# First layer of a graph network on one core: dot products by one small addition and repeated weight rows, one copy for a turned block, DVE's operations in another order

## What is computed

```python
def _cg_tp(s, v, y0, y1, w_ss, w_sv, w_vs, w_vv0, w_vv1):
    out_s = concat([w_ss * s * y0, w_vv0 * (einsum('eci,ei->ec', v, y1) / SQRT3)])
    out_v = concat([(w_sv * s)[:, :, None] * y1[:, None, :],
                    w_vs * v * y0,
                    w_vv1 * (cross(v, y1) / SQRT2)])
    return out_s, out_v
```

## Time and profile before

| | |
|---|---|
| median of 3 runs (lowest to highest) | 4406.73 us (4406.34 to 4410.24) |
| the profiled execution, its own time | 4403.17 us |
| its span | 4401.3 us |
| busy share of the span: PE, DVE, ACT, POOL | 82%, 88%, 67%, 62% |
| the first layer's loop, from the first to the last L1282 | 152.9 to 2461.0 us |
| softmax and sums | about 2470 to 2870 us |
| the second layer's loop, matmuls of L926 | 3048 to 4317 us |
| mean granted clock of PE over the span | 0.957 |

### The profile page before, as it was taken

One profiled execution on the slowest core, in us unless ns is written; L12 is line 12 of the kernel. 1 busy time (PEld: TensorE's weight loads), 2 busy tenths in 40 slices (PEclk: granted clock), 3 DMA queues, 4 the chain that ended last, 5 costly groups with the idle time before them and its releaser, 6 DMA issues. The chain is left out here.

```text
span 4401.3 us, 101790 instructions
## 1 busy us (share of the span) xinstructions
PE 3590.4 (82%) x21340; PEld 2663.2 (61%) x21340; DVE 3886.6 (88%) x13162; ACT 2961.6 (67%) x11582; POOL 2707.5 (62%) x2562
## 2 busy tenths in 40 slices
PE   4788888888888888888888477747888888888885
PEld 2678888888888888888888366634333333333334
DVE  7699999999999999999999788855888888888885
ACT  0588888888888888888888322213777776677773
POOL 0576666666666666666666022203888888888881
PEclk9999999999999999999999799956999999999997
DMA  4333333333333333333333188811444444444443
GB/s 146 104 92 88 87 86 88 86 86 88 85 86 88 85 86 88 85 86 88 85 86 88 55 215 220 213 54 53 94 90 88 91 91 88 88 92 91 89 86 92
DMA packets 313045, 426.93 MB, mean 97 GB/s; under 512 B 99333, under 2 KB 248069, under 8 KB 312613
## 3 DMA queue, kind: packets, MB, share of 16 engines
q0 software_dynamic: 141120, 225.15, 23.7%
q1 hardware_dynamic: 171876, 201.27, 14.8%
HBM read 309.10 MB, written 117.09 MB: 97 GB/s over the span
## 5 line engine op out<-in xcount | busy, mean ns | idle before, releaser
L739 POOL DMA_INDIRECT ACC<-hid_tab,idx x784 | 934.7, 1192 | 413.2 <-issue 202.6
L664 POOL DMA_INDIRECT ACC<-src_tab,idx x784 | 823.2, 1050 | 593.3 <-DMA idx<-in_idx_line 377.4
L1106 ACT ACTIVATE ACC<-TR,ACC 128x96 f32<-128x96 f32 (+1 forms) x3136 | 834.4, 392 | 252.2 <-DVE M L1532 237.8
L675 POOL DMA_INDIRECT SC<-dst_tab,idx x784 | 763.1, 973 | 239.1 <-issue 234.5
L789 PE MATMUL TR<-ident,M 128*128 128x128 f32 (+1 forms) x4704 | 650.1, 275 | 263.2 <-issue 214.5
L789 PEld LDWEIGHTS TR<-ident,M 128*128 128x128 f32 (+1 forms) x4704 | 516.3, 137 | 390.0 <-ACT M L1013 328.5
L971 ACT ACTIVATE ACC<-W,ACC 128x64 f32<-128x64 f32 x2352 | 580.9, 342 | 0.0
L838 PE MATMUL HP<-w_hv,MT 128*128 128x128 f32 x3136 | 521.5, 289 | 0.0
L984 ACT ACTIVATE MT<-TR 128x512 f32<-128x512 f32 x784 | 489.4, 624 | 0.0
L813 PE MATMUL E<-w_mv,MT 128*128 128x128 f32 x3136 | 478.9, 275 | 0.0
L926 PE MATMUL E<-M,ohE 128*128 128x480 f32 x784 | 392.7, 626 | 87.8 <-DVE M L1532 86.3
(11 more groups left out here) (220 smaller groups left out, 8216.2 us busy)
## 6 DMA issues: line engine op xcount, KB each, us to landing
h_tab<-ACC SPq DMA_DIRECT2D x392, 160.0 KB, 1.8
SC<-h_tab SPq DMA_DIRECT2D x98, 640.0 KB, 4.5
ACC<-in_e64T SPq DMA_DIRECT2D x98, 256.0 KB
agg_tab<-ACC POOLq DMA_DIRECT2D x98, 240.0 KB
ACC<-src_tab,idx POOLq DMA_INDIRECT x784
SC<-dst_tab,idx POOLq DMA_INDIRECT x784
ACC<-hid_tab,idx POOLq DMA_INDIRECT x784
sum_tab<-ACC POOLq DMA_DIRECT2D x98, 82.0 KB, 4.8
```

The source lines that it names most:

```text
L664: pool.indirect_dma_start(gat0[:, v.slot8, g, :], None, src_tab.ap(), bass.IndirectOffsetOnAxis(ap=idx[:, v.sslot, c:c + 1], axis=0))\
L675: pool.indirect_dma_start(gatd[:, v.slot8, g, :], None, dst_tab.ap(), bass.IndirectOffsetOnAxis(ap=idx[:, v.sslot, c:c + 1], axis=0))\
L739: pool.indirect_dma_start(gat1[:, v.slot8, g, :], None, hid_tab.ap(), bass.IndirectOffsetOnAxis(ap=idx[:, v.sslot, c:c + 1], axis=0))\
L1106: ins = nc.scalar.activation(WS[:, v.par, g, P * k:P * k + hi - lo], wg_[:, lo:hi], ACT.Copy, scale=yg[:, :, k:k + 1].rearrange("p a k -> ...
```

## The change

- **Dot products.** The three products are written straight into M (or M2), 96 columns. One addition adds the first 32 to the second 32 (64 elements over both groups). The third 32 stay as they are, and the weight rows that belong to the dots stand twice in `w_ms0`, `w_hs0` and `ws_val_t` (now 128 rows), so that the matmul adds the last term. `fA` and `fA2` are no longer used.
- **Turned blocks.** The turn takes columns 32 to 416, three blocks of 128. One ACT operation of 768 columns copies them.
- **Loads.** The weight rows are loaded in three parts of five loads each, 15 where there were 9.
- **DVE's order.** `products0` is cut in three: the four products, `rest_of_s0` and `rest_of_v0`; `gated`, `mixed` and `head_values` are cut in two. The order of PE and ACT stays.

```diff
-M0 = 96 + 2 * P
+M0 = C + 3 * P
-B0 = ((0, 96), (96, P), (96 + P, P))
+B0 = ((C, P), (C + P, P), (C + 2 * P, P))
...
-            for r, q in ((slice(0, C), slice(S, 96)), (slice(C, 96), slice(0, S))):
+            for r, q in ((slice(0, C), slice(S, 96)), (slice(C, S), slice(S, 96)), (slice(S, P), slice(0, S))):
                 load(by_head(w_ms0[r, 0:HL])[:, :, 0:16], by_head(a["W_alpha"][q, :]))
                 load(w_ms0[r, HL + C:ES], a["Ws_val"][q, :])
                 load(ws_val_t[:, r], a["Ws_val_T"][:, q])
-            load(w_hs0[:, :], a["Ws_vlin"])
-            load(w2s[0:64, :], rows(a["w2_ss"]))
-            load(w2s[64:96, :], rows(a["w2_vv0"]))
+                load(w_hs0[r, :], a["Ws_vlin"][q, :])
+                load(w2s[r, :], rows(a["w2_ss"] if q.start == 0 else a["w2_vv0"]))
...
-                nc.scalar.activation(dst[0:96, 0].rearrange("p g e -> p (g e)"),
-                                     tr[0:96, 0:G, :].rearrange("p g e -> p (g e)"), ACT.Copy)
-                nc.scalar.activation(dst[:, 1:3].rearrange("p k g e -> p (k g e)"),
-                                     tr[:, G:3 * G, :].rearrange("p a e -> p (a e)"), ACT.Copy).then_inc(LA[sem_done], 1)
+                nc.scalar.activation(dst[:, 0:3].rearrange("p k g e -> p (k g e)"),
+                                     tr[:, 0:3 * G, :].rearrange("p a e -> p (a e)"), ACT.Copy).then_inc(LA[sem_done], 1)
...
-                dots = ch.count(TT(fA[:, :, :, :], feat(S, (C, 3), (1, C)), wgt(160, (64, 3), (1, C)), ALU.mult))
+                dots = ch.count(TT(mid(0, (C, 3), (1, C)), feat(S, (C, 3), (1, C)), wgt(160, (64, 3), (1, C)), ALU.mult))
...
-                TT(mid(C, (S, 2), (1, S)), feat(0, (0, 2), (1, S)), wgt(C, (S, 2), (1, S)), ALU.mult)
-                ch.wait(dots)
-                nc.vector.tensor_reduce(Mt[:, :, 0:C], ax(fA[:, 0, 0, 0:1], (96, G), (1, C), (C, 3)), AX.X, ALU.add)
...
+            def rest_of_s0(v, total, parts):
+                if parts:
+                    mid, feat, wgt, dots, crosses = parts
+                    ch.wait(dots)
+                    TT(mid(C, (1, C)), mid(0, (1, C)), mid(C, (1, C)), ALU.add)
+                    TT(mid(96, (S, 2), (1, S)), feat(0, (0, 2), (1, S)), wgt(C, (S, 2), (1, S)), ALU.mult)
...
+            def mixed_sums(v, total, parts):
+                if parts:
+                    dots, crosses = parts
+                    ch.wait(dots)
+                    TT(M2[:, :, C:2 * C], M2[:, :, 0:C], M2[:, :, C:2 * C], ALU.add)
+                    ch.wait(crosses)
+                    TT(ax(M2[:, 0, 2 * P + C:2 * P + C + 1], (M0, G), (C, 3), (1, C)), fX2[:, :, :, 0, :], fX2[:, :, :, 1, :],
+                       ALU.subtract).then_inc(LA["tp"], 1)
...
             def stage0(t, total):
                 ch.restart()
-                summed = gated(t + -1, total)
+                gated(t + -1, total)
                 added = messages(t + 1, total)
-                scaled(t + -1, total, summed)
-                mixed(t + -1, total)
-                head_values(t + -2, total)
-                products0(t + 1, total, added)
+                ups = gated_up(t + -1, total)
+                parts = products0(t + 1, total, added)
+                done = summed(t + -1, total, ups)
+                scaled(t + -1, total, done)
+                mixes = mixed(t + -1, total)
+                up = head_products(t + -2, total)
+                mixed_sums(t + -1, total, mixes)
+                rest_of_s0(t + 1, total, parts)
+                head_values(t + -2, total, up)
+                rest_of_v0(t + 1, total, parts)
```

More of the change, by code:

```diff
@@ L759, in _ @@
             pe.wait_ge(s_const, 16 * n_loads)
-            nc.tensor.matmul(E1[0:96, 0, 0:C], ws_val_t[:, :], wg[:, :], start=True, stop=True).then_inc(s_wsg, 1)
+            nc.tensor.matmul(E1[:, 0, 0:C], ws_val_t[:, :], wg[:, :], start=True, stop=True).then_inc(s_wsg, 1)
             pe.wait_ge(s_bnd, 1)
@@ L810, in e1 @@
                 for g in range(G):
-                    nc.tensor.matmul(E1[:, 0, ES * g:ES * (g + 1)], MT[0:96, 0, g, :], w_ms0[:, :], start=True, stop=True)
+                    nc.tensor.matmul(E1[:, 0, ES * g:ES * (g + 1)], MT[:, 0, g, :], w_ms0[:, :], start=True, stop=True)
                     for b in range(2):
@@ L835, in hm @@
                 for g in range(G):
-                    nc.tensor.matmul(HP[:, S * g:S * (g + 1)], MT2[0:96, 0, g, :], w_hs0[:, :], start=True, stop=True)
+                    nc.tensor.matmul(HP[:, S * g:S * (g + 1)], MT2[:, 0, g, :], w_hs0[:, :], start=True, stop=True)
                     for b in range(2):
@@ L1012, in weigh2 @@
                 for g in range(G):
-                    ins = nc.scalar.activation(M2[:, g, 96:192], V2[:, g, :], ACT.Copy, scale=y_at(v, g, 0))
+                    ins = nc.scalar.activation(M2[:, g, C + P:2 * P], V2[:, g, :], ACT.Copy, scale=y_at(v, g, 0))
                 ins.then_inc(LA["m2a"], 1)
@@ L1163, in heads_of @@
                 return ax(t[:, lo:lo + 1], (LG, H), (1, w))
[L1164 to L1165 removed]
+            ch.step(TT(heads_of(la[:, 0], 0, 16), heads_of(w_ms0, 0, 16), heads_of(adot, 0, 16), ALU.mult))
+            ch.step(nc.vector.tensor_reduce(lr[:, 0, :], heads_of(la[:, 0], 0, 16), AX.X, ALU.add))
             for i, sign in enumerate((1.0, -1.0)):
[L1167 removed]
+                TS(heads_of(w_ms0, 16 + i, 1), lr[:, 0, :].rearrange("p (h a) -> p h a", a=1), 0.2 * sign, None, ALU.mult)
                 nc.vector.memset(heads_of(adot, 16 + i, 1), sign)
@@ L1182, in _ @@
             dve.wait_ge(s_wsg, 2)
-            ch.step(nc.vector.tensor_copy(w_ms0[:, HL:HL + C], E1[0:96, 0, 0:C]))
+            ch.step(nc.vector.tensor_copy(w_ms0[:, HL:HL + C], E1[:, 0, 0:C]))
             ch.step(TT(flag[:, :], E1[0:1, 1, 0:1], wide[0:1, :], ALU.add))
@@ L1283, in gated, with gated_up, summed @@
                     in1=ax(adot[:, 0:1], (0, G), (1, HL)), op0=ALU.max, op1=ALU.mult).then_inc(LA["bent"], 1)
-                up = ch.count(TT(svy[:, :, :, :], ax(E1[:, 1, 96:97], (P, G), (0, 3), (1, C)), y_of(v, 1, (1, 3), (0, C)), ALU.mult))
+            def gated_up(v, total):
+                if inside(v, total):
+                    return ch.count(TT(svy[:, :, :, :], ax(E1[:, 1, 96:97], (P, G), (0, 3), (1, C)), y_of(v, 1, (1, 3), (0, C)),
+                                       ALU.mult))
+            def summed(v, total, up):
+                if not inside(v, total):
+                    return
                 dve.wait_ge(LA["bent"], v.num + 1)
@@ L1288, in gated @@
                 ch.wait(up)
-                summed = ch.count(TT(vals[:, :, :, :], ax(E1[:, 1, 0:1], (P, G), (C, 3), (1, C)), svy[:, :, :, :], ALU.add))
-                return summed
+                return ch.count(TT(vals[:, :, :, :], ax(E1[:, 1, 0:1], (P, G), (C, 3), (1, C)), svy[:, :, :, :], ALU.add))
             def scaled(v, total, summed):
@@ L1328, in head_values @@
                 dve.wait_ge(LA["hs"], v.num + 1)
+                if v.past(1):
+                    dve.wait_ge(LA["hv"], v.num)
+                return ch.count(TT(k3(tG[:, :, :]), ax(HP[:, P + 96:P + 97], (P, G), (0, 3), (1, C)), y_of(v, 1, (1, 3), (0, C)), ALU.mult))
+            def head_values(v, total, up):
+                if not inside(v, total):
+                    return
                 if v.past(4):
                     dve.wait_ge(LA["st"][v.slot], v.slot_round(16, 4) - 16)
-                if v.past(1):
-                    dve.wait_ge(LA["hv"], v.num)
-                ch.step(TT(k3(tG[:, :, :]), ax(HP[:, P + 96:P + 97], (P, G), (0, 3), (1, C)), y_of(v, 1, (1, 3), (0, C)), ALU.mult))
+                ch.wait(up)
                 TT(hst[:, v.slot, :, S:D], ax(HP[:, P:P + 1], (P, G), (1, 96)), tG[:, :, :], ALU.add).then_inc(LA["hv"], 1)
```

44 lines of the change are left out of this document (21 added, 23 removed).

## The result

The changed kernel took 5461.6 us (median of 4 runs, 5454.0 to 5470.8), the kernel before 4408.5 us beside it (4406.3 to 4410.7). The ratio is 1.239 (1.237 to 1.241): 1053 us more. The forecast was 5185 us, 778 us more, with a range of 5035 to 5350. So the sign and, as will be seen, the places of the waits were right; the size was 277 us short.

The account below looks back on a forecast made before the run. DVE's own operations were taken to bound the kernel, 5.90 us a step. 4406.7 + 637 (ring through three engines) + 3.6 (loads) + 137 (clock drops) = 5184, rounded to 5185 us; range 5035 to 5350.

Parts of the forecast that it names:

- ring of E1: Loop on DVE and PE, bending operation through M2 subtraction, t2 and E1 to next bending: 6.82 us a step, weights in time.
- rival 2: In the loop, only the ring of E1 counts, weights in time: 6.82 us a step, 4770 us; chance 0.03.
- rival 1: In the loop, DVE's work stays the bound: 5.60 us a step, 4293 us with the loads; chance 0.04.
- What bounds the kernel before: First layer's loop: the sum of DVE's own operations, 5.90 us a step, with t2 and E1 covered by 0.20 us.
- Fewer elements: On DVE, two reductions of 192 elements become additions of 64: 0.30 us a step less.
- The weights: DVE's first product, due 0.88 us into the step, waits 0.71 us for ACT's weights, ready no earlier than 1.55.
- The cover of t2 and E1: Behind `tp` DVE keeps 1.27 us of work against a 2.41 us way; three-engine ring of 7.53 us a step, +637 us.
- The copy: On ACT, two copies of a turned block become one of 768 columns: costed at nothing, no copy standing in the ring.
- The loads: Ahead of the loop, SP issues 15 weight loads instead of 9, about 0.6 us each: +3.6 us.
- The clock: PE's holes of some 2.5 us bring clock drops: 1.05 us each, one step in three, 0.35 us a step, +137 us.
- rival 4: PE's clock drops in nearly every step: up to 1.4 us a step beyond the ring, 5590 us; chance 0.09.
- Its own signs: DVE idle 0.7 us before products, 1.2 before bending; step 7.5 to 8.1; PE holes about 2.5; clock below 1.00.

Follow-up runs that it names:

- x2: Changed kernel with DVE's operations in the order of the kernel before; small additions, wider block, loads and single copy stay: 4336.5 us, 0.983 of before.
- y11: Changed kernel with ACT's second half of the weights directly behind the first, plus 5 unread matmuls in PE's hole: 4882.2 us, 1.108 of before.
- y12: Changed kernel with 6 matmuls that nobody reads added behind W's matmuls on PE: 5154.2 us, 1.170 of before.
- x7: Changed kernel with only the four products moved back behind the sums of `mixed`: 4576.7 us, 1.037 of before.
- x8: x2 with `head_products` behind the last write into M2 and the four products between it and `head_values`: 4301.6 us, 0.976 of before.
- y10: x2 with the copy of a turned block as two ACT operations again: 4333.0 us, 0.984 of before.
- x5: Changed kernel with 4 identity matmuls that nobody reads added behind W's matmuls on PE: 5443.6 us, 1.234 of before.

## Why the prediction was right in kind and short in size

The runs split the loop's 2.68 us a step into four, each the difference of two of them:

| part | by | us a step | x 391 | forecast |
|---|---|---|---|---|
| less work on DVE | x2 - before | 5.70 - 5.90 = -0.21 | -80 | -117 |
| ring of E1, full clock | y11 - x2 | 7.10 - 5.70 = 1.40 | +549 | 1.22, +477 |
| wait for the weights | y12 - y11 | 7.79 - 7.10 = 0.69 | +271 | 0.71, +278 |
| drops | after - y12 | 8.59 - 7.79 = 0.79 | +310 | 0.35, +137 |

With the start of the loop 3.5 us later and some 2 us at the end of the span, the sum is 1054, against the measured 1053. (The forecast of the ring is 6.82 - 5.60, rival 2 less rival 1.)

**What bounds the kernel before**: right. Taking work off DVE with the order kept (x2) shortens the step, and taking the cover away (x7, after) lengthens it.

**Fewer elements**: the size was off by a third, and it didn't matter in the sum, since the ring set the step. The small addition is 0.13 us, as the prediction took it; that is partly luck, for its slope (192 elements 0.27, 144 in the mean 0.225) comes to 0.15 for 64. The rest went mostly to a pair of operations in which the second waits for the first: 0.45 us for L1351 to L1360 in x2. In x8 other operations fill that wait. Its step is down by 5.90 - 5.61 = 0.29, but that is no measure of DVE's work, since the ring bounds it.

**The weights**: right in place and size. In the step shown DVE stood 0.64 us for ACT's L970, over the loop 245.2 / 376 = 0.65, where 0.71 was forecast.

**The cover of t2 and E1**: right. The ring in the step of the changed kernel that is shown above, by the same terms as the prediction's: weights and handover 1.61 (forecast 1.59), products 0.88 (0.88), reduction 0.21 (0.21), `vals` 0.48 (0.38), V2 0.39 (0.38), `mixed` 0.93 (0.90), `head_products` 0.27 (0.27), small addition 0.13 (0.13), subtraction 0.35 (0.34), t2 and E1 3.73 (2.41), handover 0.04 (0.04). The sum is 9.02, the distance from 1005.72 to 1014.74. Without the drop's 1.32 it is 7.70 against the forecast of 7.53, and the largest of the small misses is `vals` to V2, 0.48 where 0.38 was carried over from another pair. The mean at full clock is 7.79, since a quarter of the steps take 7.96 to 8.11, two in each turn of the loop's body; the prediction had no term for them. It had said of `head_products` that it has no slack against ACT's scalars and had costed it at nothing. It starts 0.04 us after they land (1010.22 in the step above; ACT's L1020 lands at 1009.93 + 0.25 = 1010.18), which makes `mixed` 0.93 instead of 0.90. Taken together 0.26 us a step, 102 us, of the miss.

The Trainium skill ("VectorE: DVE Perf Modes", section "The DRAIN you can't avoid") says that a semaphore between two DVE operations costs nothing extra. The prediction gave it 0.11 us a step. The runs went further from it: 0.48 us from `vals` to V2 in the changed kernel and 0.45 from L1351 to L1360 in x2, against 0.26 between L1351 and an operation that doesn't use its result in x8. In all these pairs the second also reads the first's result; what the semaphore costs alone was not tried. The measurement decides.

**The copy**: costed at nothing, and it was nothing (y10 against x2), where DVE bounds the step. In the ring it was not tried.

**The loads**: 3.6 us forecast. The first weight operation of DVE starts 3.8 us later than at the 55.59 of the earlier trace rows:

```profile
59.35 0.17 DVE L1145 TENSOR_SCALAR w_rbf<-w_rbf 16x32 f32<-16x32 f32 x1 [4.06 <-DMA w_hv<-in_Wv_vlin]
```

**The clock**: this is the step that failed. "I take one step in three, between none and two in three" put the rate in the middle of a range for which no row spoke, and the price at 1.05 us a drop. Measured: a drop in 0.59 of the steps, at 9.14 - 7.80 = 1.34 us each. The product is 0.79 us instead of 0.35, 173 us more, and the same 0.79 is the difference between after and y12. The rate is near the upper end of its bounds. The result lies among the times of rival 4, many drops (5400 to 5590), but only together with the ring's own miss: the drops alone cost less than the 0.9 us a step at which it begins. The argument held against it, that a drop takes away the hole that the next one would need, was half right. After a step with a drop the next hole was 2.17 us in the median instead of 2.46, and 94 of 222 such steps were followed by another drop, against 131 of 157 steps without one. So a drop makes the next one about half as likely and no less: it lies on t2 and E1, which are in the ring, it lengthens the step, and a hole of some 2 us stays. "A drop starts when PE gets work again" was too simple as well. In the step shown the turn still ran at full clock (clock 1.00 until 1011.5, 0.50 from 1012), and so it did in 160 of the 223 steps with a drop. In x5 a drop began in the hole itself (clock 0.88 from 1024.0 to the turn at 1024.38). That is one reason why a drop cost less than the 2.2 us of the upper bound. As the prediction said, a step over 8.4 us means the drops were sized too small: it was 8.59.

**Its own signs**: idle time of 0.64 ahead of the first product (0.7 said), 1.18 ahead of the bending at full clock (1.2), holes of 2.45 on PE (2.5), a clock below 1.00. Only the step left the 7.5 to 8.1 us that it gave.

## What to carry to other kernels

Before operations are moved on a saturated engine, write down for each of its semaphores what stands between the write and the next wait that needs its answer; that is the cover, and a trace shows it only as the absence of idle time. Read the waits start to start as well: idle time behind the landing of the operation before leaves short ones out (x8). Here 2.68 us of work covered a way of 2.41 us, and four small products taken out of it cost 885 us. Where a move opens a hole on PE ahead of the matmuls that everything waits for, count the drops of the clock as likely, and at a good half of what those matmuls would cost at half clock (here 1.2 to 1.5 of 2.2 us); and where the hole can't be closed, six matmuls that nobody reads, placed in it, gave 307 us back.
